# Adjacency blocks times node features in float32: one level's visits cut into tiles of 32 columns, four side by side, in place of two of 64

## What is computed

```python
h = jnp.maximum(_layernorm(x, axis=-1), 0.0)
# layer 0: T1 = adj @ h; T2 = 2 * (adj @ T1) - h; T3 = 2 * (adj @ T2) - T1
x = x + (h @ w[0] + T1 @ w[1] + T2 @ w[2] + T3 @ w[3] + bias0)
h = jnp.maximum(_layernorm(x, axis=-1), 0.0)
# layer 1: expmap(h) = tanh(|h|) * h / (|h| + eps); logmap(y) = atanh(|y|) * y / (|y| + eps)
x = x + logmap(adj @ expmap(h)) @ kernel + bias1
```

## Time and profile before

| | us |
|---|---|
| median of 3 runs | 1865.16 (1864.85 to 1866.59) |
| the profiled execution | 1866.52 |
| its span, first to last instruction | 1864.7 |
| TensorE, line 502 and 504 (BOTH, later sweeps) | 756.4 and 756.4 |
| TensorE, line 482 and 484 (BOTH, first sweep) | 420.8 and 420.8 |
| TensorE, line 516 (AGAIN) | 344.1 |
| TensorE, line 532 (OWN) | 69.1 |

### The profile page before, as it was taken

The page is one execution under the profiler, slowest core; times in us unless marked ns, Lnnn a source line. Parts: engine busy times, 40 slices in busy tenths (PEclk is TensorE's granted clock), DMA queues, the critical chain, the costliest instruction groups (busy, mean ns, idle before and its releaser), DMA issues.

```text
span 1864.7 us, 22367 instructions
## 1 busy us (share of the span) xinstructions
PE 1833.7 (98%) x9620; PEld 806.1 (43%) x9620; DVE 421.8 (23%) x877; ACT 120.9 (6%) x226; POOL 24.1 (1%) x39
## 2 busy tenths in 40 slices
PE   7999999999999999999999999999999999999996
PEld 4444444444444444444444444344444444444443
DVE  7111111111121123000000002432321222122147
ACT  1000000000000000000000001211000000000014
POOL 0000000000000000000000000000000000000000
PEclk9999999999999999999999999999999999999998
DMA  9999999999999985888888785899999999999993
GB/s 380 420 421 421 421 421 415 389 387 395 385 383 376 387 307 220 319 295 297 294 303 303 265 300 180 348 372 374 383 377 389 391 380 378 400 395 373 412 406 144
DMA packets 94832, 662.30 MB, mean 355 GB/s; under 512 B 11408, under 2 KB 13712, under 8 KB 14608
## 3 DMA queue, kind: packets, MB, share of 16 engines
q1 hardware_dynamic: 93744, 660.64, 90.8%
q10 hardware_dynamic: 992, 0.23, 0.1%
HBM read 658.74 MB, written 2.10 MB: 354 GB/s over the span
## 4 chain that ended last, share of the span: by engine, by line
PE 95%; DVE 2%; DMA 1%; issue 1%; SPq 1%; ACT 0%; DVEq 0%
PE row_bank L502 36%; PE work_bank L482 19%; PE work_bank L516 16%; PE row_bank L471 12%; PE row_bank L504 3%; PE own_bank L532 3%; PE work_bank L484 3%; PE turned L587 2%; DMA ring<-adj_blocks 1%; DVE nodes L897 0%; DVE partial L758 0%; SPq L407 0%; PE work_bank L556 0%; SPq L418 0%; PE own_bank L543 0%
## 5 line engine op out<-in xcount | busy, mean ns | idle before, releaser
L504 PE MATMUL row_bank<-ring,nodes 128*64 128x512 f32 x1728 | 756.4, 592 | 0.0
L502 PE MATMUL row_bank<-ring,nodes 128*64 128x512 f32 x1728 | 756.4, 592 | 0.0
L502 PEld LDWEIGHTS row_bank<-ring,nodes 128*64 128x64 f32 x1728 | 236.4, 137 | 437.3 <-issue 434.5
L484 PE MATMUL work_bank<-ring,nodes 128*64 128x512 f32 x936 | 420.8, 592 | 0.0
L482 PE MATMUL work_bank<-ring,nodes 128*64 128x512 f32 x936 | 420.8, 592 | 0.0
L516 PE MATMUL work_bank<-ring,nodes 128*64 128x512 f32 x1456 | 344.1, 595 | 0.3 <-DVE nodes L862 0.2
L471 PE MATMUL row_bank<-ring,nodes 128*64 128x512 f32 x1112 | 270.3, 597 | 6.3 <-DMA ring<-adj_blocks 6.3
L504 PEld LDWEIGHTS row_bank<-ring,nodes 128*64 128x64 f32 x1728 | 236.4, 137 | 0.0
L482 PEld LDWEIGHTS work_bank<-ring,nodes 128*64 128x64 f32 x936 | 127.9, 137 | 218.8 <-issue 218.8
L516 PEld LDWEIGHTS work_bank<-ring,nodes 128*64 128x64 f32 x1456 | 124.8, 138 | 170.2 <-issue 168.7
L758 DVE TENSOR_TENSOR partial<-partial,work_bank 128x512 f32<-128x512 f32 x148 | 101.3, 686 | 327.1 <-PE work_bank L516 326.0
(11 more groups left out here) (101 smaller groups left out, 511.2 us busy)
## 6 DMA issues: line engine op xcount, KB each, us to landing
ring<-adj_blocks SPq DMA_DIRECT2D x626, 1024.0 KB, 7.6
out<-resid SPq DMA_DIRECT2D x16, 128.0 KB, 1.8
resid<-x SPq DMA_DIRECT2D x7, 256.0 KB, 11.5
resid<-x SPq DMA_DIRECT2D x2, 128.0 KB, 3.5
w_raw<-cheb_weight ACTq DMA_DIRECT2D x2, 64.0 KB, 7.9
bias<-cheb_bias ACTq DMA_DIRECT2D x1, 32.0 KB, 2.8
bias<-hyp_bias ACTq DMA_DIRECT2D x1, 32.0 KB, 3.9
w_raw<-hyp_kernel ACTq DMA_DIRECT2D x2, 16.0 KB, 8.9
```

Of the source, the lines that this page charges most:

```text
L484: done = nc.tensor.matmul(bank[EVEN, :], nodes[:, c * C + k, B, :], data[:, k, :], start=k == 0, stop=k == C - 1)
L502: nc.tensor.matmul(bank[ODD, :], nodes[:, c * C + k, A, :], data[:, k, :], start=first and k == 0, stop=last and k == C - 1)
L504: done = nc.tensor.matmul(bank[EVEN, :], nodes[:, c * C + k, B, :], data[:, k, :], start=first and k == 0, stop=last and k == C - 1)
```

## The change

In a FRESH visit, and only there, each matmul of 64 columns becomes two of 32. The four tiles are at columns 0, 32, 64 and 96: chunks k = 0 and 2 go to the first two tiles (features 0 to 31 and 32 to 63), k = 1 and 3 to the last two. Every feature's sum lands in the same PSUM partition as before, and from the same products. Each chunk of data is streamed twice, once for each part. The position in the array is given by hand. The flags `start` and `stop` and the signal at the end of the visit stay as they are. All other steps keep their tiles of 64 columns.

```diff
                     for k in range(C):
-                        half = (ODD, EVEN)[k % 2]
-                        done = nc.tensor.matmul(bank[half, :], nodes[:, c * C + k, A, :], data[:, k, :],
-                                                start=first and k < 2, stop=last and k >= 2)
+                        for part in range(2):
+                            quarter = (k % 2 * 2 + part) * F // 2
+                            features = slice(part * F // 2, (part + 1) * F // 2)
+                            done = nc.tensor.matmul(bank[quarter:quarter + F // 2, :], nodes[:, c * C + k, A, features],
+                                                    data[:, k, :], start=first and k < 2, stop=last and k >= 2,
+                                                    tile_position=(0, quarter))
                     done.then_inc(s_visit, 1)
```

## The result

The changed kernel takes 1903.13 us (median; 1901.47 to 1904.47), against 1865.01 us for the kernel before on the same chip: a ratio of 1.0203, with a 95% interval of 1.0185 to 1.0220. It is 38 us slower. The forecast was 53 us more, 1918, in a range of 1864 to 1963.

The account below looks back on a forecast made before the run. TensorE, never free in the first sweep's changed stage, was taken to bound the kernel. Streaming, loads and issue counted 0; 265 passages x 0.20 us gave 53 us, so 1918 us, in a range of 1864 to 1963.

Parts of the forecast that it names:

- The bound: First sweep's FRESH stage: TensorE has no free time, so any loss reaches the end one for one; DMA close behind.
- Streaming at 0: FRESH visits: four tiles side by side take four steps of 0.428 us, 1.71 us as before, so no cost.
- the estimate of 6.7 us: FRESH visits: packed tiles starting 4 ns apart, 3 x 4 ns on each of 4 x 139 rounds; the sum has 0.
- Loads and issue at 0: FRESH visits: doubled weight loads and instructions stay covered, even in row 0's tightest rounds, so no cost.
- The bound of 45 ns an instruction, 13 us: Row 0's rounds: if issue cover failed to this rate, 1 us more over some 13 rounds; taken as 0.
- The change of cut: First sweep: 265 passages between FRESH and other kinds, each draining the array, 0.20 us each, 53 us; chance 0.62.
- No price: First sweep's passages between tile widths: they overlap as now and cost nothing, 1865 us; chance 0.20.
- Serial: FRESH visits: four tiles don't run side by side, 3.42 us a visit, 2103 us or 2156 with passages; chance 0.15.
- a cut by hand might not be obeyed: FRESH visits: engine treats each half as one tile, so 32-column parts follow each other, 238 us; within the 0.15 rival.
- Faster: FRESH visits: 32-column matmuls stream faster or DMA limits; DMA caps the gain at 3% of the stage; chance 0.03.

Follow-up runs that it names:

- the order of pairs at 64 columns: Kernel before, with first-sweep FRESH visits after row 0 coming two at a time, then two of the others: 1864.32 us, ratio 0.9995.

## Why the prediction was right, point by point

**The bound.** That TensorE has no free time in this stage and that a loss there reaches the end undiminished held: 37.2 us were lost before the last FRESH visit, and 38.1 at the end. DMA's share fell (0.99 to 0.97 between 60 and 640 us), and no wait for a block was added.

**Streaming at 0.** Right. Four visits in a row take 4 x 1.716 us and one change. With all visits cut in four, the kernel after row 0 runs at its old pace. The Trainium skill, "TensorE: Matmul & The Clock Gate", Part 3, has packed tiles start some 4 ns apart, and the estimate of 6.7 us that was worked out from it isn't seen: the first four starts of a visit lie within some 0.03 us, but each tile repeats at its own 0.43 us, so such a stagger isn't paid in each round.

**Loads and issue at 0.** Right for this change, but the cover was thinner than the prediction had it. I read the rate from H_TERM, 15 ns an instruction. That holds for a burst of 0.47 us. Over 37 us, kernels with every matmul of row 0 cut in four got no better than 37 / (652 + 655) = 28 ns on average, with pauses of up to 1.9 us. The changed kernel asks for 37 / (484 + 487) = 38 ns there, and has none of them. The bound of 45 ns an instruction, 13 us, was too dear.

**The change of cut.** The mechanism was right: no weights are loaded across it, the next matmul starts late, and the price hangs on the number of changes (265, 153, 272, 234), not on visits or instructions. The Trainium skill, "TensorEngine Tiling (Array Packing)", section "Key Properties", states that a change of the tiling mode drains TensorE; these runs agree with it, with 0.145 us for each change. That the array is empty in between can't be seen itself, as the ends of matmuls are modelled. What was mis-sized is the term of 0.20 us; it is 0.145. I built it from the overlap of one record, 592 - 428 = 164 ns, and 0.03 us of load. The array is ready for the next cut sooner than the record ends (202.66 + 0.59 = 203.25, next start 203.18): the last start of one cut to the first start of the next is 0.52 us, so 0.09 us more than the usual step of 0.43, where I had 0.16. The load before the first matmul isn't seen as a gap of its own, but the first step is longer, by 25 ns into 32 columns (a record of 617 in place of 592) and by 52 ns into 64 (644). Where the upper half's first load comes late without any change of width, in the kernel with BOTH sorted by tile, the record is 643 ns too, so this part belongs to the load. 0.09 + 0.025 or 0.09 + 0.052 are 0.12 and 0.14 us; what the 0.01 to 0.02 us that are left are isn't shown. 265 x 0.055 us too much is the 15 us by which the forecast was high, so the mechanism and the range held, and the price of one change was put 0.2 / 0.145 = 1.4 times too high.

**The rivals.** *No price* fell with the first changes in the timeline. *Serial* fell: four streams of float32 run at once, and the reach is three for each tile, which was enough; the rival had counted it over the whole queue. That a cut by hand might not be obeyed fell with the records of 32 columns. *Faster* had no mechanism and none appeared; even the kernel without any change of cut is no faster than the one before. The kernel before stays the best of all that ran, with the order of pairs at 64 columns equal to it.

## What to carry to other kernels

Where two layouts of an operation fill the array equally, as here (1.71 us a visit in either), cutting one finer brought nothing, and each passage between tiles of different widths cost about 0.14 to 0.17 us: the next matmul started 0.09 us late, and no weights were loaded ahead. Count the passages in the instruction order, not the operations; keep one width across steps that alternate, or put steps of the same width next to each other. When a price is read from a trace, starts are measured and ends of matmuls are modelled: take it from one start to the next.

## What the runs showed of the hardware that wasn't expected

- A change of tile width costs about as much between 128 and 64 columns (0.169 us) as between 64 and 32 (0.129 to 0.145 us).
- TensorE starts a later instruction of a free tile past three waiting ones of a busy tile and no more (with eight ahead for the busy half, the free one stood idle from 60.98 to 62.70 us), and at least past nine that wait for three tiles, three each (four starts within 0.04 us).
- Where small matmuls follow one another for tens of us, TensorE stood still for 0.8 to 1.9 us at a time, six times in some 40 us, with no semaphore to wait for, once the instructions asked for came to 20 ns each over a round (128 in 2.6 us). At 38 ns each there was none. In the two kernels with these pauses, 9.5 and 11 us were lost beyond the changes of cut, of which the pauses are 7.2 and 7.9; what causes them stays open.
